# An LSTM recurrence whose gate sums move from SBUF to unused columns of its PSUM banks

## The reference

```python
def lstm_scan(x, h0, Wx, Wh, b):                     # x: 8 x 512 x 512
    xW = jnp.einsum('ntd,dg->ntg', x, Wx) + b        # g = 4 * 512
    def step(carry, xw_t):
        prev_h, prev_c = carry
        a = xw_t + prev_h @ Wh
        i = jax.nn.sigmoid(a[:, :Hdim]); f = jax.nn.sigmoid(a[:, Hdim:2*Hdim])
        o = jax.nn.sigmoid(a[:, 2*Hdim:3*Hdim]); g = jnp.tanh(a[:, 3*Hdim:])
        next_c = f * prev_c + i * g
        next_h = o * jnp.tanh(next_c)
        return ((next_h, next_c), next_h)
...
x = x + lstm(x, cond, Wx, Wh, b)
proj = conv(x, taps = cond) @ Wp + bp                # folded into one weight, wpk
state = decay * state + dt * softplus(B_t) * (x @ Ws + bs)
x = x + (tanh(C_t) * state) @ Wo + bo
```

## Time and profile before

| what | value |
|---|---|
| median of 3 timed runs | 1887.65 us (1887.31 to 1887.77) |
| span of the profiled execution, first to last instruction | 1887.5 us |
| TensorE, matmuls busy | 1806.9 us, 96% |
| TensorE, weight loads busy | 1418.6 us, 75% |
| VectorE busy | 1387.4 us, 74% |
| ScalarE busy | 1120.3 us, 59% |
| GpSimd busy | 340.0 us, 18% |
| granted TensorE clock, mean | 0.996 |

### The profile page before, as it was taken

The page is one execution under the profiler, slowest core; times in us unless marked ns, Lnnn a source line. Parts: engine busy times, 40 slices in busy tenths (PEclk is TensorE's granted clock), DMA queues, the critical chain, the costliest instruction groups (busy, mean ns, idle before and its releaser), DMA issues.

```text
span 1887.5 us, 124428 instructions
## 1 busy us (share of the span) xinstructions
PE 1806.9 (96%) x52834; PEld 1418.6 (75%) x52834; DVE 1387.4 (74%) x7266; ACT 1120.3 (59%) x4565; POOL 340.0 (18%) x1544
## 2 busy tenths in 40 slices
PE   6888999999999999999999999999999999999987
PEld 3666777777777777777777777777777787888875
DVE  8787667777776777767777776777767777777776
ACT  5555565665655656566565655656556565656564
POOL 1111111111111111111111111111111111111111
PEclk9999999999999999999999999999999999999999
DMA  6111111111111111111111111111112111211110
GB/s 236 54 46 36 48 48 44 51 53 48 50 52 44 57 46 54 49 45 59 46 51 55 49 50 48 57 41 54 54 38 66 44 48 54 60 38 56 44 35 25
DMA packets 112292, 100.75 MB, mean 53 GB/s; under 512 B 20225, under 2 KB 86069, under 8 KB 110710
## 3 DMA queue, kind: packets, MB, share of 16 engines
q1 hardware_dynamic: 111448, 90.70, 15.8%
q10 hardware_dynamic: 288, 2.10, 0.3%
HBM read 50.77 MB, written 41.94 MB: 49 GB/s over the span
## 4 chain that ended last, share of the span: by engine, by line
PE 76%; ACT 9%; DVE 8%; issue 2%; POOL 2%; DMA 1%; SPq 0%; DVEq 0%; ACTq 0%
PE recA L562 28%; PE recB L569 17%; PE pw L521 13%; PE pbc L646 13%; ACT act L851 4%; DVE tr L974 4%; ACT recA L777 3%; DVE pre L983 2%; POOL h L488 2%; DVE hz L1009 2%; PE pw L505 1%; ACT tc L866 1%; PE pu L619 1%; PE po L666 1%; DMA wpk<-in_L_cond_Wh_dram 1%
## 5 line engine op out<-in xcount | busy, mean ns | idle before, releaser
L851 ACT ACTIVATE act<-pre 128x64 f32<-128x64 f32 (+1 forms) x1024 | 255.6, 250 | 709.5 <-DVE pre L983 701.8
L569 PE MATMUL recB<-wlo,hz 128*32 128x128 f16 x16352 | 577.0, 219 | 0.4 <-issue 0.3
L569 PE MATMUL recB<-whi,hz 128*32 128x128 f16 x16352 | 576.8, 219 | 0.2 <-issue 0.2
L562 PE MATMUL recA<-whi,hz 128*16 128x256 f16 x8176 | 515.3, 274 | 54.2 <-DVE hz L1009 46.0
L562 PE MATMUL recA<-wlo,hz 128*16 128x256 f16 x8176 | 511.9, 273 | 0.0
L569 PEld LDWEIGHTS recB<-whi,hz 128*32 128x32 f16 x16352 | 437.5, 97 | 10.0 <-issue 0.4
L569 PEld LDWEIGHTS recB<-wlo,hz 128*32 128x32 f16 x16352 | 437.5, 97 | 3.0 <-issue 0.7
L562 PEld LDWEIGHTS recA<-whi,hz 128*16 128x16 f16 x8176 | 199.9, 88 | 282.5 <-DVE hz L1009 264.4
L974 DVE STREAM_TRANSPOSE tr<-recA 128x256 f32<-128x256 f32 x512 | 230.2, 450 | 228.4 <-PE recA L562 227.2
L646 PE MATMUL pbc<-yt,wpk 128*128 128x256 f32 (+1 forms) x1216 | 332.6, 381 | 0.0
L488 POOL TENSOR_TENSOR h<-osc,tc 128x16 f32<-128x16 f32 x1024 | 228.2, 223 | 451.0 <-ACT tc L866 451.0
(11 more groups left out here) (162 smaller groups left out, 2120.7 us busy)
## 6 DMA issues: line engine op xcount, KB each, us to landing
xw_rows<-xs SPq DMA_DIRECT2D x128, 256.0 KB, 2.4
seed<-xw_rows SPq DMA_DIRECT2D x1008, 32.0 KB, 2.0
xn<-in_x_dram SPq DMA_DIRECT2D x32, 256.0 KB
out_dram<-ot SPq DMA_DIRECT2D x32, 256.0 KB, 3.1
seed<-in_L_cond_Wh_dram ACTq DMA_DIRECT2D x2, 1024.0 KB, 6.9
wpk<-in_L_cond_Wh_dram SPq DMA_DIRECT2D x2, 1024.0 KB, 12.1
wlo<-in_L_cond_Wx_dram SPq DMA_DIRECT2D x2, 1024.0 KB, 13.5
xs<-in_L_cond_Wx_dram SPq DMA_DIRECT2D x1, 1024.0 KB, 9.7
```

The source lines that it names most:

```text
L562: ins = pe.matmul(rec[0][32 * j:32 * j + 2 * NB, 0:256].rearrange("p (c f) -> p c f", c=2), h[:, 2 * NB:4 * NB], w[:, k, :, :].rearrange(" ...
L569: ins = pe.matmul(rec[1][32 * j:32 * j + 32, 0:128], h[:, 2 * NB * (1 - c):2 * NB * (1 - c) + 32], w[:, k, 4 * (2 + c) + j, :], start=Fals ...
L851: act_eng.activation(act[q][:, q:G, :].rearrange("p g n -> p (g n)"), pre[q][:, q:G, :, :].rearrange("p g c b -> p (g c b)"), ACT.Tanh, sc ...
```

## The change

The tile `pre` is no longer two tiles in SBUF but two views of 64 columns, one in each bank of the recurrence: columns 256 to 319 of `recA` and 128 to 191 of `recB`. The sums of lines 983 and 980 are written there by VectorE, and the tanh of line 851 reads them there. The o gate's sum of half 1 (line 987) gets a small SBUF tile of its own, `preo`, which `gate_o` reads. Since the tanh now reads the banks, TensorE waits ahead of step 1's x rows for the tanh of step 0 (`s_tg`) where it waited for the transposes (`s_tr`). In all other steps its matmuls come behind the seeds, which ScalarE writes after the tanh. Every engine issues the same instructions in the same order as before; only the operands' places differ.

```diff
-        pre = [sb(f"pre{h}", [128, G, 2, NB]) for h in range(2)]
...
+        preo = sb("preo", [128, 2, NB])
...
+        pre = [rec[q][:, 256 - 128 * q:320 - 128 * q].rearrange("p (g c b) -> p g c b", g=G, c=2) for q in range(2)]
...
             for t in range(END):
                 if t == 1:
                     for half in range(2):
-                        pe.wait_ge(s_tr[half], 1)
+                        pe.wait_ge(s_tg[half], 1)
                         first_rows(1, half)
...
             def gate_o(t):
                 act_eng.wait_ge(s_addo, t + 1)
-                act_eng.activation(act[1][:, 0, :], pre[1][:, 0, :, :].rearrange("p c b -> p (c b)"), ACT.Tanh,
+                act_eng.activation(act[1][:, 0, :], preo[:, :, :].rearrange("p c b -> p (c b)"), ACT.Tanh,
                                    scale=gain).then_inc(s_tgo, 1)
...
             def add_o(t):
-                dve.tensor_tensor(pre[1][:, 0, :, :], tr[1][:, 0, :, 0, :], tr[1][:, 0, :, 1, :],
+                dve.tensor_tensor(preo[:, :, :], tr[1][:, 0, :, 0, :], tr[1][:, 0, :, 1, :],
                                   ALU.add).then_inc(s_addo, 1)
```

## The result

The changed kernel takes 1877.01 us (median of 4 runs, 1875.23 to 1879.16) against 1887.71 us for the one before (4 runs): ratio 0.9942, 95% interval 0.9928 to 0.9956. The forecast was 1876.7. Later groups of runs gave the same kernel 1879.00 us beside 1888.62, and 1878.27 beside 1886.57.

A forecast was written before the change was run, and what follows sets the result against it. The recurrence's own chain was taken to bound 397 steps, not TensorE's work. Terms of -6 and -24 ns a step, limited by margins, gave -11.0 us from 1887.65: 1876.7 us, range 1870 to 1894.

The forecast's parts named there:

- The bound: Whole step: the recurrence's own chain sets 397 of 509 counted starts, TensorE's side work the other 112.
- rival D: Whole kernel: the chain doesn't bound, TensorE's 96% busy does; nothing moves, 1887.6 us; chance 0.12 together with B.
- The tanh from PSUM: ScalarE's tanh of the gates, two per step: reading PSUM instead of SBUF takes 38 ns less each, ends 0 and -46.
- The write to PSUM: VectorE's sums, two per step: writing PSUM costs +14 ns each, allowed 0 to +60.
- Rival A: Sums 0 and 1: VectorE's write to PSUM is dear; at +60 ns, +18.0 us, 1905.7 us; chance 0.22.
- B: Sums and tanh: the two prices cancel at a write of 33 to 43 ns; about 1887 us; chance 0.12 together with D.
- second pair: Sum 1 and tanh of gates 1: counts in full, +14 - 38 = -24 ns a step.
- C: VectorE's sums: write to PSUM costs 0, -44 ns a step, -16.1 us, 1871.5 us; inside the main case's 0.66.
- The sum along the step: Chain inside one step: both pairs of sum and tanh together change it by -6 - 24 = -30 ns.
- first pair: Sum 0 and tanh of gates 0: gain lost except at most 6 ns, because sum 1 also waits for transpose 1.
- the count of margins: 397 chain-set steps: each gains the smaller of 30 ns and its margin before TensorE's side work, 11.0 us in all.
- The wait ahead of step 1: TensorE's two waits before step 1's x rows, now for step 0's tanh: charged 0, at most 0.1 us.

The follow-up runs named there:

- half 0 alone: Only half 0's sums moved to PSUM, half 1's kept in SBUF, against the kernel before: 1887.28 us against 1887.57, ratio 1.0000.
- half 1's state: Changed kernel with half 1's state also written to PSUM for its tanh from step 1 on: 1868.90 us, 9.4 us under the changed kernel.

## Why the prediction was right

**The bound.** That the chain of the recurrence sets most steps, against a chain view that says TensorE 76%, held: a delay of 83 ns cost 39.4 us (rival D is out), and 363 steps gave back 10.8 us.

**The tanh from PSUM.** Predicted -38 each; measured -32 and -33 by their rows. From start to start the gain was larger: the tanh of the state follows the tanh of gates 1 after 107 ns, where it was 149; 8 of these 42 ns go again, since the tanh of the state itself takes 207 ns and not 199. The Trainium skill (Perfetto Trace Analysis, "Optimizing Scalar/DVE Operations") has 42 ns between ScalarE's overheads on SBUF and PSUM, and calls them engine-busy times: the trace agrees in the distance from start to start, and not in the length of the row.

**The write to PSUM.** Predicted +14, with 0 to +60 left open; measured +9 for sum 0 (224 to 233), +8 for sum 1 where nothing else changed (202 to 210), and +6 for the state. Rival A, a dear write, is out; so are B, since the second pair's net is -25 and not near 0, and C, whose -16.1 us lies outside the interval. The same section of the Trainium skill has 65 ns between VectorE's overheads on SBUF and PSUM; that is seen neither in the read of the earlier trace rows nor in these writes.

**The sum along the step.** Predicted -30: -6 and -24. The second pair gave 8 - 33 = -25, where two errors of 5 to 6 ns cancelled, one in the price of the write and one in the gain of the tanh. The first pair's gain is lost as predicted, and more fully: of the 6 ns that I left it, 1 to 2 are seen in the step with half 0 alone, none beside half 1 (3512 ns with half 0 and without), and none in the time. The measured step is 26 ns shorter than before (3.512 us, where 3.51 was forecast), and the wait for `hz` fell by 13.0 us, where 11 was. The term of 30 was 4 ns too large.

**From the step to the time.** 26 ns by the count of margins are 9.5 us; the runs' difference is 10.7 (8.3 to 13.6 by the interval of the ratio). The forecast of -11.0 lies in that too. With my terms corrected the count gives 9.5, so the closeness of 1876.7 to 1877.01 is in part luck: the runs can't tell the two apart, and the two later groups had the changed kernel 10.2 and 9.1 us under the kernel before by the ratio. That the profile's span and the median were "the same to 0.15" did no harm, since the forecast was taken from the median.

**The wait ahead of step 1.** I charged 0 and allowed 0.1 us. At the full clock that held: step 1 starts 0.05 us behind the low part in spite of the wait. What I had not thought of is that the lower clock can fall on the same stretch; then step 1 starts 0.24 to 0.45 us later. No run shows a cost in the time; the kernel before with that wait alone bounds it at 1.7 us.

## What to carry to other kernels

An operand that VectorE writes and ScalarE reads was through 23 to 26 ns sooner each time it moved from SBUF to PSUM, but the kernel had the gain only where that hand-over was on the path that sets the step; ask of each hand-over what else its consumer waits for. Two paths that end together must both be shortened: half 1's state paid 9 us because its low part was the later one at recA's third quarter. A busy TensorE row proves no bound; an inserted delay of known size does, if its true length is read from start to start and not from its own row.

## What the runs showed of the hardware that was not expected

- An instruction's row can grow when it starts sooner: sum 1 into SBUF took 203 ns, and 208 when the product ahead of it no longer waited. The tanh of the state took 199 ns, and 207 when it started 42 ns sooner behind the tanh of gates 1. A row's length must be compared in the same surroundings.
- A two-column memset has a row of 60 ns and held VectorE for 10.
- The start-up of 13 of the 14 profiles has one stretch at the lower of TensorE's two granted clocks: 6.8 us long at about 20 us (the kernel before, for one) or 3.4 us long at 45 to 47 us (the changed kernel's first profile, there with recA matmuls of up to 0.42 us in place of 0.27). Both places occur in kernels with and without the edit. The changed kernel's third profile has none before 1833 us.
- Seven of the 14 profiles have a stretch of 3.4 us at the lower clock that begins in step 503, near 1830 us (in the kernel with the 83 ns delay, at 1877). There step 503 takes 4.4 to 5.1 us; in the other seven it takes 3.5. So such a stretch costs 0.9 us or more there, and it is one part of the spread of the runs. It is seen in six of the nine kernels and groups with half 1's sums in PSUM, and in one of the five others; whether the change makes it likelier is not shown.
